# Two layers of masked graph attention: who makes the first layer's key masks, and in how many steps GpSimd multiplies

## The reference

```
qkv = layer_norm(x, g1, be1) @ w_qkv
scores = einsum("nhd,mhd->hnm", q, k) * SCALE
scores = where((adj != 0)[None], scores, -inf)
attn = softmax(scores, axis=-1)
out = einsum("hnm,mhd->nhd", attn, v).reshape(n, 128)
x = x + out @ w_proj + b_proj
x = x + gelu(layer_norm(x, g2, be2) @ w1 + b1) @ w2 + b2
```

## Time and profile before

| | us |
|---|---|
| median of three runs | 3502.21 |
| lowest, highest | 3500.7, 3504.06 |
| the profiled execution | 3504.94 |
| its span, first to last instruction | 3503.2 |
| attention of the first layer | about 207 to 1675 |
| attention of the second layer | about 1990 to 3385 |

### The profile page before, as it was taken

How to read it: one execution, slowest core, us unless ns; L and a number is a source line. 1 busy time by engine, 2 the same in 40 slices (tenths; PEclk the granted TensorE clock), 3 DMA queues, 4 the chain that set the end, 5 groups by cost and what they waited for, 6 DMA issues and landing times.

```text
span 3503.2 us, 71453 instructions
## 1 busy us (share of the span) xinstructions
PE 3351.8 (96%) x22292; PEld 1483.3 (42%) x22312; DVE 2840.6 (81%) x8964; ACT 2479.3 (71%) x3620; POOL 2484.2 (71%) x1476
## 2 busy tenths in 40 slices
PE   6899999999999999999778999999999999999978
PEld 3444444343434343432544444444444444444326
DVE  6888888898989888981347999999999999999514
ACT  4448788787879797978333177777777777777753
POOL 1057878787878878889210188888888888888960
PEclk9679999999999999999888599999999999999989
DMA  3568787878797878874223365555565555555532
GB/s 132 179 213 268 237 286 234 285 229 292 223 299 221 290 234 275 262 243 143 79 79 122 109 184 172 184 173 183 173 184 172 185 172 185 172 185 171 149 90 70
DMA packets 487031, 677.56 MB, mean 193 GB/s; under 512 B 57952, under 2 KB 279264, under 8 KB 482272
## 3 DMA queue, kind: packets, MB, share of 16 engines
q1 hardware_dynamic: 486224, 672.88, 61.1%
q10 hardware_dynamic: 432, 0.10, 0.0%
HBM read 508.67 MB, written 166.20 MB: 193 GB/s over the span
## 4 chain that ended last, share of the span: by engine, by line
PE 80%; issue 5%; DVE 3%; DMA 2%; POOL 1%; SPq 1%; ACT 1%; POOLq 1%; DVEq 0%; ACTq 0%
PE PS L466 28%; PE PS L449 18%; PE PS L473 16%; PE PS L479 14%; DVE spill L817 2%; PE PS L425 2%; PE PS L527 1%; POOL arena L966 1%; ACT arena L682 1%; DMA q_t<-max_dram 1%; POOLq L943 1%; PE PS L597 0%; DMA max_dram<-stage_t 0%; SPq L307 0%; DVE arena L777 0%
## 5 line engine op out<-in xcount | busy, mean ns | idle before, releaser
L817 DVE CUSTOM_DVE_ANT_0 spill<-PS,mask_n 128x512 bf16<-128x512 f32 x4096 | 2587.9, 687 | 279.3 <-PE PS L449 271.3
L682 ACT ACTIVATE arena<-PS 128x512 f32<-128x512 f32 (+1 forms) x3072 | 2133.3, 739 | 615.3 <-PE PS L473 371.6
L966 POOL TENSOR_TENSOR arena<-arena,mask 128x1024 int32<-128x1024 int32 x896 | 2131.8, 2379 | 484.1 <-ACT arena L682 415.0
L449 PE MATMUL PS<-k_t,q_t 48*128 48x512 f32 x4096 | 1694.2, 542 | 14.2 <-DMA q_t<-q_dram 12.1
L473 PE MATMUL PS<-q_t,k_t 50*128 50x512 f32 x4096 | 1258.1, 485 | 11.8 <-DMA q_t<-max_dram 9.0
L479 PE MATMUL PS<-arena,idb 64*128 64x512 bf16 x4304 | 1150.5, 389 | 0.0
L466 PE MATMUL PS<-arena,v_sb 128*32 128x512 f32 x8192 | 1094.8, 606 | 8.2 <-POOL arena L966 7.9
L449 PEld LDWEIGHTS PS<-k_t,q_t 48*128 48x128 f32 x4096 | 627.3, 195 | 942.4 <-DVE pmax L817 898.6
L473 PEld LDWEIGHTS PS<-q_t,k_t 50*128 50x128 f32 x4096 | 594.5, 188 | 209.1 <-issue 112.1
L479 PEld LDWEIGHTS PS<-arena,idb 64*128 64x128 bf16 x4304 | 310.4, 94 | 376.5 <-PE PS L479 230.7
L817 DVE DVE_READ_ACCUMULATOR2_ANT pmax<- 128x1 f32 x4096 | 340.5, 83 | 0.0
(11 more groups left out here) (51 smaller groups left out, 845.2 us busy)
## 6 DMA issues: line engine op xcount, KB each, us to landing
mask<-m_dram SPq DMA_DIRECT2D x768, 256.0 KB, 2.7
mask_n<-mn_dram SPq DMA_DIRECT2D x768, 128.0 KB, 2.8
adj_in<-in_adj SPq DMA_DIRECT2D x256, 256.0 KB, 4.4
mask<-in_adj_t SPq DMA_DIRECT2D x256, 256.0 KB, 4.1
m_dram<-mask SPq DMA_DIRECT2D x256, 256.0 KB, 3.6
mn_dram<-mask_n SPq DMA_DIRECT2D x256, 128.0 KB, 4.4
mt_dram<-arena SPq DMA_DIRECT2D x256, 128.0 KB, 3.5
arena<-mt_dram SPq DMA_DIRECT2D x256, 128.0 KB, 2.7
```

Of the source, the lines that this page charges most:

```text
L449: pe.matmul(ps_a[:, (L * NSC + n) % A_BANKS, :], q_t[r0:r0 + KROWS, gb % Q_SLOTS, pair, q * P:(q + 1) * P], k_t[r0:r0 + KROWS, pair, mb * ...
L682: nc.scalar.activation(p_buf[:, t % P_SLOTS, heads, :], ps_b[:, heads, :], ACT.Exp, scale=SCALE).then_inc(exped[part], 1)
L817: dve.tensor_tensor_reduce(spill[:, bank, :], ps_a[:, bank, :], mask_n[:, v % N_SLOTS, :], 1.0, LOWEST, ALU.subtract, ALU.max, pmax[:, p % ...
L966: pool.tensor_tensor(p, p, m, ALU.mult).then_inc(p_masked, 1)
```

## The change

In the even passes of the first layer the steps go by threes. With r = `s % 3`:
- r = 0 is not pooled, r = 1 and r = 2 are (`pooled`). That is 21 of the 32 steps of a pass in place of 16.
- For the keys of steps with r = 2 (10 in a pass) ACT makes the addend (`mask_keys`), in the way in which it makes the rows' masks, from the clamped 0/1 mask. It stands in ACT's order behind the exponentials of the step two earlier (an r = 0 step) and waits for POOL's clamp. POOL makes the clamp alone there. `t_made` becomes two semaphores.
- The addend changes its sign, since an exponential is positive: POOL multiplies by the other sign, and the identity is negative.

```diff
         def pooled(L, t):
-            return L > 0 or t // MT % 2 == 1 or t % 2 == 1
+            return L > 0 or t // MT % 2 == 1 or t % MT % 3 > 0
...
+        def by_act(t):
+
+            return t % MT % 3 == 2
+
+        ADDENDS = [[sum(made(0, u) and by_act(u) == who for u in range(t)) for t in range(STEPS + 1)] for who in range(2)]
+
+        def addend_made(eng, t):
+            eng.wait_ge(t_made[by_act(t)], ADDENDS[by_act(t)][t + 1])
...
-                        sp.wait_ge(t_made, MADE[t - M_SLOTS + 1])
+                        addend_made(sp, t - M_SLOTS)
...
-                sp.wait_ge(t_made, MADE[t + 1])
+                addend_made(sp, t)
...
-                    pe.wait_ge(t_made, nb * MT + s + 1)
+                    addend_made(pe, nb * 2 * MT + s)
...
+            def mask_keys(t):
+                nb, s, slot = t // (2 * MT), t % MT, t % M_SLOTS
+                act.wait_ge(mask01_made, MADE[t + 1])
+                if nb > 0:
+                    act.wait_ge(scored[0], t - MT + 1)
+                    act.wait_ge(mt_stored, nb * MT * 16)
+                nc.scalar.activation(mask_t[:, s, :], mask01[:, slot, :].bitcast(U32), ACT.Exp,
+                                     bias=far[:], scale=MASKED).then_inc(t_made[1], 1)
...
                     for part in (1, 0, 2) if pooled(L, t) and scores_before(t + 1) > scores_before(t) else (0, 1, 2):
                         exp_heads(L, t, part)
+                    if t + 2 < STEPS and made(L, t + 2) and by_act(t + 2):
+                        mask_keys(t + 2)
...
                 pool.tensor_scalar(m, m.bitcast(U32), 1.0, 0.0, ALU.min, ALU.max).then_inc(mask01_made, 1)
+                if by_act(t):
+                    return
...
-                pool.tensor_scalar(mask_t[:, s, :], m, -MASKED, MASKED, ALU.mult, ALU.add).then_inc(t_made, 1)
+                pool.tensor_scalar(mask_t[:, s, :], m, MASKED, -MASKED, ALU.mult, ALU.add).then_inc(t_made[0], 1)
...
-    ident = give("ident", np.eye(P, dtype=ml_dtypes.bfloat16))
+    ident = give("ident", -np.eye(P, dtype=ml_dtypes.bfloat16))
```

More of the change, by code:

```diff
@@ L157, in gnn_kernel @@
         adjt_loaded = [sem(f"adjt_loaded_{i}") for i in range(M_SLOTS)]
-        n_made, mask01_made, t_made, p_masked = sem("n_made"), sem("mask01_made"), sem("t_made"), sem("p_masked")
+        n_made, mask01_made, t_made, p_masked = sem("n_made"), sem("mask01_made"), (sem("t_made_pool"), sem("t_made_act")), sem("p_masked")
         m01_stored, mt_stored = [sem(f"m01_stored_{i}") for i in range(M_SLOTS)], sem("mt_stored")
@@ L700, in mask_rows @@
                                      bias=far[:], scale=MASKED).then_inc(n_made, 1)
+            def mask_keys(t):
[6 more added lines that the diff above has]
+                                     bias=far[:], scale=MASKED).then_inc(t_made[1], 1)
             def attend(L):
                 visits = [v for v in range(NV) if rows_made(L, v)]
[L704 to L707, removed]
+                at = 0
+                while at < len(visits) and visit_step(visits[at]) < 3:
+                    mask_rows(visits[at])
+                    at += 1
                 for t in range(STEPS):
@@ L712, in attend @@
                         exp_heads(L, t, part)
-                    while made < len(visits) and visit_step(visits[made]) - 3 < t + 1:
-                        mask_rows(visits[made])
-                        made += 1
+                    if t + 2 < STEPS and made(L, t + 2) and by_act(t + 2):
+                        mask_keys(t + 2)
+                    while at < len(visits) and visit_step(visits[at]) - 3 < t + 1:
+                        mask_rows(visits[at])
+                        at += 1
                 keep_o(L, 2 * NB - 1)
```

## The result

The changed kernel takes **3573.0 us** (median of four runs, 3566.6 to 3576.9) against 3502.1 of the kernel before: a ratio of 1.020, 95% interval 1.018 to 1.022. It is 71 us slower; 82 were forecast. The span of the profiled execution grew by 68.1 us, from 3503.2 to 3571.3.

A forecast was written before the change was run, and what follows sets the result against it. PE was taken to set the pace before the change. Rings and pass ends 66, rows' masks 8.5 and clock 8 sum to +82 us: 3587 profiled, median 3584 us, 2.3% slower, range 3566 to 3614.

The forecast's parts named there:

- a ring through POOL and ACT: Even passes: exponentials, two multiplications with masks between, clamp, addend, exponentials form a loop of 9.67 us for three steps.
- Part 1: Even passes: five fewer unpooled steps save PE 2.5 us a pass; three steps would take 8.63 us if PE paces.
- Part 2: POOL's row of work after an r = 1 step's exponentials: the clamp for the next r = 2 step done at 6.91 us.
- Part 3: ACT's addend waits for POOL's clamp until 7.05 us, so the r = 1 step's exponentials end at 9.67 us.
- The first ring: Start of even passes other than the first: three multiplications come together, POOL's clamp is late, +2.1 us.
- The first pass: First even pass: nothing ahead of the first clamp; +0.1, nine rings +7.1, last steps +0.2, together 7 us.
- The rows' masks: On ACT for steps 24 and 27 of seven even passes, no longer hidden: 14 x 0.61 = 8.5 us.
- The clock: PE's clock stays at 0.8 us idle, falls in the first ring and those with rows' masks: about 14 rings, 8 us.
- The clock falls in all rings: Rival: PE's idle time lowers its clock in every ring, half of the other 66 hit, +19, 3603 us; chance 0.12.
- The cover holds: Rival: POOL's clamp is done before ACT reaches the addend, PE sets the pace, 3481 us; chance 0.08.
- SP's waits: SP's store of the r = 2 addend and loads behind it wait for ACT; over 4 us of room, set at nothing.

The follow-up runs named there:

- e1: Changed kernel, but POOL makes the clamp for the r = 2 step one step earlier, ahead of the r = 2 multiplication: 3505.0 us, 1.001.
- e4: Changed kernel with POOL's clamp of the r = 2 steps done twice in place (80 clamps more): 3629.8 us, 1.037.
- e2: Changed kernel's new steps (two of three pooled), but all addends made by POOL and none by ACT: 3526.1 us, 1.007.
- e5: Changed kernel with the rows' mask ahead of the addend on ACT where both stand behind the same step's exponentials: 3556.4 us, 1.016.
- e6: e1 with the r = 2 mask loaded one step earlier and the rows' mask after r = 2 steps made one step ahead: 3510.4 us, 1.002.
- e8: e1 with the rows' mask after r = 2 steps made one step ahead, and seven mask buffers for six: 3492.5 us, 0.9971.

## Why the prediction was right

**The mechanism and the sign were right**: a ring through POOL and ACT, in which PE waits, and which costs although every engine has idle time. Shown by e1 (order alone, -66 to -68 us), e4 (each added us of POOL goes through, in rings with and without a fall of the clock) and e2 (more work for POOL, less time).

**Part 1** held: with the ring gone, three steps take 8.66 to 8.7 us.

**Part 2** held: from multiplication to clamp 2.34 us, clamp and addend 1.48, multiplication to clamp 2.34 in the timeline of POOL, against 2.33, 1.49 and 2.33:

```profile
624.56 0.63 POOL L969 TENSOR_SCALAR mask<-mask 128x512 int32<-128x512 uint32 x1
...
628.38 1.20 POOL L969 TENSOR_SCALAR mask<-mask 128x512 int32<-128x512 uint32 x2
```

**Part 3**, the ring's length, was mis-sized by a little: 9.56 in place of 9.67. Two terms make this up. ACT takes notice of POOL's clamp in about 0.03 us (clamp ended 629.02, addend 629.04), where 0.14 was taken from the other direction, and exponentials with their scores there take 1.98, not 2.01; the addend's 0.63 in place of 0.61 goes the other way. Over 72 rings this is 8 us of the 82.

**The first ring** of a pass was read right from the earlier trace rows: +2.0 measured, +2.1 forecast.

**The first pass** came out near its forecast by luck: 6.9 us measured, against 7 and another 1.2 for its rows' masks. The prediction gave its first ring no price of its own, but E went from step 1 to step 4 in 11.49 us where the rings behind it take 9.48; and it counted the steps of before at 5.92 us in two (79.9 us from step 1 to step 28), where step 2 alone took 4.68 and the stretch 81.9. These two nearly cancel.

**The rows' masks** cost what was forecast: 1.21 us in two rings of each pass, 8.5 us, shown by e5.

**The clock** was the term that was too large. Eight us were set for 14 rings. In the trace of after it fell in three first rings, about 0.5 us each, and not once behind the 14 waits of 1.26 to 1.37 us in the rings with rows' masks. Its other two falls are at the starts of odd passes, as are the three of the kernel before. The forecast had drawn a line between 1.10 and 1.22 from the earlier trace rows; there is none at a length of wait alone. Here is a wait of 2.39 us with no fall and one of 1.24 with a fall (timeline of PE; then the busy times of the 4 us around each, with the granted clock as the third number from the end):

```profile
1282.27 0.50 PE L482 MATMUL PS<-q_t,k_t 50*128 50x512 f32 x2 [2.39 <-DMA q_t<-max_dram]
```
```profile
404.20 1.07 PE L475 MATMUL PS<-arena,v_sb 128*32 128x512 f32 x8 [0.49 <-POOL arena L988]
...
406.93 0.79 PE L482 MATMUL PS<-q_t,k_t 50*128 50x512 f32 x2 [1.24 <-ACT arena L691]
```
```profile
1282.00:1286.00 4.00, 3.73 (x28) 1.72 (x28) 2.06 (x7) 2.74 (x5) 1.06 (x2) 1.00 0.91 237
406.00:410.00 4.00, 3.07 (x14) 1.54 (x18) 2.26 (x7) 2.83 (x5) 2.59 (x2) 0.62 0.86 257
```

Nor is it the wait of 0.49 us ahead of the second one: all seven first rings have the same two waits, and the clock fell in three of them. What decides stays open.

The sum of these, 82 - 8 - 6.5 = 67.5, comes near the 67.6 of the trace; that it agrees to the tenth is luck, since the smaller differences above are not in it. The medians of the runs differ by 71.

**The rivals.** "The clock falls in all rings" did not come with waits of 0.74 us. In e4, with 1.47 us, the clock did go up and down, 35 times. The Trainium skill's page "TensorE: Matmul & The Clock Gate" describes such swings under "A second HAM failure mode: psum-queue depth-cycling"; the changed kernel does not show them in its rings and e4 does. The page has them lower the throughput, and in e4's rings they cost next to nothing, since PE was not what set the pace. "The cover holds" was wrong for the changed kernel and is what e1, e6 and e8 are: its 3481 was too low by 11 even for the best of them.

**SP's waits** were set at nothing, with over 4 us of room for the load ahead of a clamp. In the changed kernel that held (the list of waits has nine waits of POOL for loads there, 8.8 us in all, less than before). In e1 and e6 it did not: a clamp that comes a step earlier has used that room up.

## What to carry to other kernels

Before giving an instruction to an engine that is idle a third of the time, write down what it waits for, what stands behind it, and whether the engine it waits for itself waits for that: if so the price is the length of that loop, not the instruction's 0.6 us. Here the loop cost 71 us, and making its one input a step earlier gave 66 to 68 back. An input made earlier needs its own load earlier too, so look for the buffers before counting the gain, and when a backlog is the cause, take work out of it and not a single wait.

## What the runs showed of the hardware that was not expected

- In the changed kernel's trace ACT's addend starts 0.03 us after the end of the POOL clamp that it waited for, in all 75 places, while POOL's multiplication starts 0.13 to 0.14 us after ACT's last exponential: the price of a handover was not the same in the two directions.
- The length of a PE wait alone did not tell whether the granted clock fell. In the changed kernel it stayed at the 2.4 GHz level behind waits of 1.88 and 2.39 us (1476.7 and 1282.3) and fell to 1.2 GHz behind 1.24 us, with the same pair of waits (0.49 and 1.24 us) followed by a fall in three places of seven.
- A fall of the clock need not cost time: in e4 a ring with a fall took 10.30 us and the one ahead of it, without a fall, 10.31.
